# Two orders of work exchanged in the first stage of a four-layer kernel: scores ahead of projections, sigmoids ahead of masked copies

## What is computed

```python
q = (x @ wq.T).reshape(B, T, H, HD)
kv = (x @ wkv.T).reshape(B, T, H, 2 * HD)
nb_k, nb_v = ...   # keys and values of the 16 tokens before
tau = sigmoid(einsum('bthd,bthwd->bthw', q, nb_k) / SCALE)
msg = einsum('bthw,bthwd->bthd', tau, nb_v)
y = x + msg.reshape(B, T, D) @ wo.T
out = (y - mu) * rsqrt(var + LN_EPS) * gamma + beta
```

## Time and profile before

| | us |
|---|---|
| three runs | 1069.3, 1071.47, 1071.88 |
| median | 1071.47 |
| the profiled execution, its own time | 1073.75 |
| its span | 1071.9 |
| PE busy (share) | 887.4 (83%) |
| DVE busy | 671.8 (63%) |
| ACT busy | 572.0 (53%) |
| POOL busy | 492.8 (46%) |

### The profile page before, as it was taken

One profiled execution on the slowest core, in us unless ns is written; L12 is line 12 of the kernel. 1 busy time (PEld: TensorE's weight loads), 2 busy tenths in 40 slices (PEclk: granted clock), 3 DMA queues, 4 the chain that ended last, 5 costly groups with the idle time before them and its releaser, 6 DMA issues.

```text
span 1071.9 us, 21820 instructions
## 1 busy us (share of the span) xinstructions
PE 887.4 (83%) x8032; PEld 712.3 (66%) x8032; DVE 671.8 (63%) x2014; ACT 572.0 (53%) x1033; POOL 492.8 (46%) x893
## 2 busy tenths in 40 slices
PE   1777778276999999998657888998849999999995
PEld 0766667165888888877535565655537888878785
DVE  3566665366588888875329998989856155180622
ACT  1434343133667666665366897977826354362631
POOL 1366665322255455434368899999840002020111
PEclk9856565555789999999867998888959999999998
DMA  9100000110000000000020000000000000000000
GB/s 307 39 10 15 10 15 17 40 50 1 2 6 12 7 12 6 12 12 11 10 84 1 1 1 1 1 1 0 2 0 1 1 1 20 1 20 0 1 20 20
DMA packets 30707, 20.67 MB, mean 19 GB/s; under 512 B 2960, under 2 KB 28952, under 8 KB 30368
## 3 DMA queue, kind: packets, MB, share of 16 engines
q1 hardware_dynamic: 25984, 12.59, 4.1%
q10 hardware_dynamic: 4640, 6.99, 1.9%
HBM read 13.28 MB, written 6.29 MB: 18 GB/s over the span
## 4 chain that ended last, share of the span: by engine, by line
PE 57%; POOL 19%; DVE 10%; issue 6%; ACT 5%; DMA 1%; ACTq 1%; POOLq 0%; SPq 0%; DVEq 0%
PE ps L1108 12%; PE ps L1109 9%; PE ps L1110 9%; PE ps L1121 6%; PE ps L1183 6%; POOL prod L529 5%; POOL term L514 4%; PE ps L1442 3%; PE ps L1176 2%; PE ps L1127 2%; PE ps L1103 2%; POOL c_ln_rs L119 2%; DVE wall L985 2%; POOL a_ln_rs L113 1%; PE ps L1160 1%
## 5 line engine op out<-in xcount | busy, mean ns | idle before, releaser
L112 POOL TENSOR_TENSOR d_ln_ve<-d_ln_mv,eps 128x4 f32<-128x4 f32 x16 | 3.2, 202 | 238.7 <-DVE d_ln_mv L106 238.7
L1108 PE MATMUL ps<-h_h,wh_h 128*128 128x512 f32 x256 | 99.6, 389 | 0.0
L1109 PE MATMUL ps<-h_h,wh_l 128*128 128x512 f32 x256 | 99.6, 389 | 0.0
L1110 PE MATMUL ps<-h_l,wh_h 128*128 128x512 f32 x256 | 99.6, 389 | 0.0
L1183 PE MATMUL ps<-w_e,he 128*128 128x128 f32 x512 | 83.3, 300 | 5.1 <-ACT he L618 4.8
L1121 PEld LDWEIGHTS ps<-mov,hbd 32*128 32x128 f32 x2048 | 85.4, 251 | 0.0
L1121 PE MATMUL ps<-mov,hbd 32*128 32x32 f32 (+1 forms) x2048 | 83.1, 324 | 0.0
L618 ACT ACTIVATE he<-ps,pp 128x256 f32<-128x256 f32 x128 | 59.8, 472 | 43.1 <-PE ps L1110 38.1
L1183 PEld LDWEIGHTS ps<-w_e,he 128*128 128x128 f32 x512 | 73.1, 211 | 7.7 <-ACT he L618 7.0
L529 POOL TENSOR_TENSOR prod<-bcT 16x256 f32<-16x256 f32 (+7 forms) x128 | 69.0, 567 | 6.3 <-ACT bcT L738 6.3
L1086 DVE TENSOR_TENSOR d_y<-ps,w_s 128x512 f32<-128x512 f32 x8 | 5.5, 691 | 102.5 <-PE ps L1442 102.5
(11 more groups left out here) (244 smaller groups left out, 2624.0 us busy)
## 6 DMA issues: line engine op xcount, KB each, us to landing
x<-x SPq DMA_DIRECT2D x32, 128.0 KB, 1.8
x<-in_x SPq DMA_DIRECT2D x16, 128.0 KB
w_h<-in_w_h ACTq DMA_DIRECT2D x2, 1024.0 KB, 8.7
xB<-x SPq DMA_DIRECT2D x32, 64.0 KB
x<-xB SPq DMA_DIRECT2D x32, 64.0 KB
out_x<-x SPq DMA_DIRECT2D x8, 256.0 KB, 2.3
w_m<-in_w_m ACTq DMA_DIRECT2D x3, 256.0 KB, 5.3
xB<-in_w_e ACTq DMA_DIRECT2D x1, 512.0 KB
```

Of the source, the lines that this page charges most:

```text
L1108: pe.matmul(dst, a_h, b_h, start=start, stop=True, skip_group_check=True)
L1109: pe.matmul(dst, a_l, b_h, start=False, stop=True, skip_group_check=True)
L1110: return pe.matmul(dst, a_h, b_l, start=False, stop=True, skip_group_check=True)
```

## The change

On ACT the sigmoids of sequence n now stand ahead of the masked copies of n+1. On PE the scores of n stand ahead of the projection of n+1. The fourth bank of the scores of n holds the transposed input of n+1 until ACT and DVE have made `xh` and `xl` from it, so the wait for `a_xl` now stands ahead of the scores too. No instruction besides this wait is added, and none is removed.

```diff
--- before.py
+++ after.py
@@ -589,10 +589,6 @@
 
 
             def step_a(n, l, have):
-                if have(1):
-                    act.wait_ge(S["a_qk_ps"], n + 2)
-                    four_heads(1 - l, 4 * (1 - l) + 1, S["a_hbd"])
-                    act.activation(mov[1 - l][:, :], ps[:, 4 * (1 - l), 0:NT], ACT.Copy).then_inc(S["a_qT"], 1)
                 if have(0):
                     for k in range(2):
 
@@ -600,6 +596,10 @@
                         act.activation(tau[l][:, 2 * k:2 * k + 2, :],
                                        ps[:, 4 * l + 2 * k:4 * l + 2 * k + 2, 0:NBLK * SPAN], ACT.Sigmoid,
                                        scale=ATT_SCALE).then_inc(S["a_tau"], 1)
+                if have(1):
+                    act.wait_ge(S["a_qk_ps"], n + 2)
+                    four_heads(1 - l, 4 * (1 - l) + 1, S["a_hbd"])
+                    act.activation(mov[1 - l][:, :], ps[:, 4 * (1 - l), 0:NT], ACT.Copy).then_inc(S["a_qT"], 1)
                 if have(2):
                     transposed(l, 4 * (1 - l) + 3, n + 3, S["a_t_ps"], S["a_xh"])
                 if have(0):
@@ -1130,14 +1130,14 @@
 
             def step_a(n, l, have):
                 o = 1 - l
-                if have(1):
-                    pe.wait_ge(S["a_xl"], n + 2)
-                    project(o, 4 * o, wa_h, wa_l, S["a_qk_ps"], S["a_v_ps"])
                 if have(0):
                     pe.wait_ge(S["a_qT"], n + 1)
                     pe.wait_ge(S["a_hbd"], n + 1)
 
                     pe.wait_ge(S["a_vbd"], n + 1)
+                    if have(1):
+
+                        pe.wait_ge(S["a_xl"], n + 2)
                     for g in range(G):
 
                         pe.matmul(bank(l, g, 0, NBLK * SPAN), rep[heads(g), :], band[heads(g), :], start=True, stop=True)
@@ -1147,6 +1147,9 @@
                             last = score(l, bank(l, g, SPAN * j, SPAN * j + w), g, j, w)
                             if j == NBLK - 1 and g % 2 == 1:
                                 last.then_inc(S["a_s_ps"], 1)
+                if have(1):
+                    pe.wait_ge(S["a_xl"], n + 2)
+                    project(o, 4 * o, wa_h, wa_l, S["a_qk_ps"], S["a_v_ps"])
                 if have(2):
                     if have(-1):
```

## The result

The changed kernel takes 1067.65 us (median of 12 runs, 1064.1 to 1072.2), the kernel before, run beside it, 1070.86 us (12 runs, 1067.29 to 1074.64). The ratio is 0.9963, with a 95% interval of 0.9946 to 0.9980: 2 to 6 us less. The forecast was 1069.0 against 1071.47, a ratio of 0.9977.

What follows compares the result with a forecast made beforehand. Two loops were taken to compete: DVE with POOL (10.00 us a step) and PE's path, longer at low clock. Start 37.75 plus steps 134.1 gave 171.8 against 174.32, -2.5 us, end 0: 1069.0 us, range 1065.3 to 1073.8.

Steps and rivals of the forecast that it cites:

- The wait on `xl`: PE's wait, now ahead of the scores too, costs nothing new: the projection ahead of them already waited for it.
- the sigmoids hide under the projection: At low clock ACT's sigmoids run under PE's projection, taking 1.51 us and two handovers off the path, adding 0.69 of transposes.
- T+10.1: With T the start of `t_y`: when PE's path would allow the next `t_y` at low clock, instead of T+10.94.
- ACT's copies behind the sigmoids: Masked copies end about T+7.9, before `msgT` is needed at T+8.4; cost nothing, covered by PE's messages.
- `values` is the price: On DVE at low clock vT waits until T+6.17 for the later projection, statistics start at T+7.78, step becomes 10.51 us.
- `t_z` and vbd come apart: At low clock POOL's `t_z` ends before DVE's vbd begins, paying back about half of what `values` waits.
- rival C: Slower: low clock throughout and vbd keeps 1.49 us, so steps of 10.78 us, 1075.4 us in all; chance 0.12.
- The clock: Scores get less high clock: 5 of 13 steps at 10.00 us, 8 at 10.51, 134.1 us against 135.7.
- Rival B: The high clock stays: all 13 steps at 10.00 us, 1064.3 us in all; chance 0.2.
- The base: The thirteen steps of the kernel before, taken from one profile as 135.70 us, 10.44 us each.
- The start: First scores need only the second sequence's `xl`, so the first `t_y` comes at 37.75 against 38.62: 0.87 us earlier.
- The end: From the `t_y` at 174.32 to the last at 191.87: no change expected, bounds -0.6 and +0.3 us.

Runs made afterwards that it cites:

- e4: Changed kernel with `values` moved on DVE between the third statistics and `t_o`; 1061.49 us, ratio to before 0.9904.
- e2: Kernel before with only ACT's new order (sigmoids ahead of the masked copies), PE's order kept; ratio to before 1.0029.
- e3: Changed kernel with vT reading a constant tile, so `values` wait for nothing (attention's values left out); ratio to before 0.9932.
- e9: Changed kernel run again without alteration, for a second profile; ratio to before 0.9973.
- e11: Against e4: vT moved ahead of the third statistics, vbd alone left behind them; 1068.4 us, ratio to before 0.9957.
- e8: Changed kernel with five extra matmuls on PE behind each output product; ratio to before 0.9964.
- e10: Repetition of e4, unaltered; 1060.77 us, ratio to before 0.9891.
- e7: Kernel before with only `values` moved on DVE behind the third statistics; ratio to before 0.9993.
- e6: Changed kernel with the first stage's projections cut from nine matmuls to three; ratio to before 0.9945.
- e5: Kernel before with the first stage's projections cut from nine matmuls to three; ratio to before 0.9952.

## Why the prediction was right, and where its terms were off

The forecast of -2.5 us lies in what was measured (2 to 6 us less), and 1067.65 us lies in the range of 1065.3 to 1073.8. That range also holds the 1071.47 of no change, so it says little by itself; the steps say more:

- **The wait on `xl` costs nothing**, and **the sigmoids hide under the projection**: as told. The output is ready early, and the wait before `t_y` is gone from the loop. PE's path was even shorter than I reckoned: 9.7 to 9.8 us in e4 where I had T+10.1. I had counted the projection to the end of its last matmul (2.28 us) and the transposes with 0.69, where 2.09 and 0.56 pass until the next instruction starts (111.82, 113.91, 114.47).
- **ACT's copies behind the sigmoids** cost nothing: PE's wait for `msgT` is 0.50 us as before. e2 shows what they cost when PE's order does not cover them.
- **`values` is the price**: as told, shown by e3. vT at T+6.25 against T+6.17, the statistics at T+7.88 against T+7.78, the low-clock step 10.48 to 10.59 against 10.51. That `t_z` and vbd come apart was right: vT is 1.57 us later than before, the third statistics only 0.6. With it rival C (10.78 us) fell. One reading behind it was wrong, though not the number: `t_z` does not lengthen vbd. It is POOL's product before it that does (last section), and that one, too, is over in the long step.
- **The clock**: 5 of 13 short steps expected, 7 and 6 found; 134.1 us expected and 133.5 measured in both profiles. Rival B, all steps at 10.0, did not come. Whether the change itself shifts the share of the high clock stays open: 6 and 9 of 13 steps were short before, 7 and 6 are now.
- **The base was mis-sized.** The thirteen steps of before took 135.7 us in the profile I had and 133.3 in a second. The steps' share of the gain, from the means of two profiles each, is 134.5 - 133.5 = 1.0 us and not 1.6, and the 2.4 us between the two profiles of before are more than that. What is firm is the length by kind: a low-clock step behind a high-clock one took 10.94 us (10.60 to 10.71 where its projection began at the high clock) and takes 10.5 to 10.6. A second low-clock step in a row took 10.40 (from 163.92) and takes 10.49 (e9, from 57.38): there the change gains nothing.
- **The start was mis-sized**: 0.87 us expected, 12.90 - 11.22 = 1.7 us measured (12.89 - 11.34 = 1.6 in the second pair). I had carried over the output's 1.26 us, the projection's 2.28 and the transposes' 0.69. The clock rose before the output product, which took 0.75 us to `t_y`; the transposes began 2.09 us after the projection, and the messages 0.56 us after them. In e11, where the clock did not rise, the start is 11.74, still 1.2 us less than before.
- **The end was mis-sized**: 0 expected, with -0.6 as bound; 24.29 and 22.45 us measured against 24.66 and 25.06, 0.4 and 2.6 less, on average 1.5. The last step, from the fifteenth `t_y` to the sixteenth, was PE's and took 8.48 us in both profiles of before; it takes 6.94 in both of the changed kernel, by DVE and POOL's chain. The last scores start at T+9.18 of the fourteenth `t_y` in the first profile (178.83 against 169.65), near my T+9.35, and at T+6.92 in e9 (177.31 against 170.39), both times at the high clock. At the low clock (e11) they leave a last step of 7.84 us and an end of 24.95, no shorter than before. So the gain at the end hangs on the clock. Four more profiles of the new order, e3, e4, e8 and e10, have ends of 22.28 to 22.74.

So start, steps and end gave about 1.6, 1.0 and 1.5 us, 4.1 in all, against 0.9, 1.6 and 0. Three of the four microseconds came once, from filling and draining the pipeline, and not from the loop, where I had looked for most of the gain. That the sum was off by only 1.6 us is partly luck: the steps were taken too high, the start and the end too low. The split itself rests on two profiles each; only the start is the same in both. I had given 0.36 to a gain of 0.3% or more and 0.52 to no such difference; 0.37% and 0.27% were measured, one on either side.

## What to carry to other kernels

Where two loops of nearly the same length compete, shortening one is worth only the difference between them; here that was 0.4 us a step at best, and only where a low-clock step followed a high-clock one. But it can be the condition for the next step: the same DVE move was worth nothing before (e7) and 6 to 9 us on top of the change (e4, e10). Look for such a follow-up in the engine that now waits, and place work of VectorE so that it does not start just ahead of a small instruction of GpSimd on which the chain hangs (e11). Reckon the start and the end of a pipeline as carefully as its steps: with sixteen sequences they gave more than the loop. And take a second profile of the kernel before, if the argument rests on the share of steps at either clock.

## What the runs showed of the hardware

- A small GpSimd instruction (128x2) that starts 0.17 us after a VectorE product with two SBUF inputs took 1.08 us instead of 0.20 and ended with it (e11). That agrees with what the Trainium skill says (SBUF — State Buffer, "Who interferes with whom"): the first to start keeps the port, the other blocks. The other way round it depends on GpSimd's instruction. In e4 its power (128x2, L113, 92.53, 0.71 us) started ahead of vbd (92.55), which took 1.25 us, hardly more than the 1.22 alone, where the rule would give some 1.9 (an estimate: 0.69 until the power ends, then 1.22).
- A GpSimd product (128x256) that is still running does hold vbd up. In e6 both neighbours of vbd come at other times than in the kernel before:

```profile
91.04 0.72 POOL L428 TENSOR_TENSOR t_zn<-t_zn,rows 128x256 f32<-128x256 f32 x1 [0.93 <-DVE t_zn L135]
...
91.65 1.23 DVE L801 TENSOR_TENSOR vbd<-vT,vmask 128x1024 f32<-128x1024 f32 x1
...
91.84 1.62 POOL L429 TENSOR_TENSOR t_z<-t_zn,rows 128x256 f32<-128x256 f32 x1
```

```profile
101.05 0.72 POOL L428 TENSOR_TENSOR t_zn<-t_zn,rows 128x256 f32<-128x256 f32 x1 [0.93 <-DVE t_zn L135]
...
101.57 1.28 DVE L801 TENSOR_TENSOR vbd<-vT,vmask 128x1024 f32<-128x1024 f32 x1
```

L428 ends 0.11 us after vbd's start in the first, 0.20 in the second and 0.42 in the kernel before (137.92 against 137.50), and vbd takes 1.23, 1.28 and 1.49 us, against 1.22 alone. `t_z` runs beside it all three times and is itself slowed (1.62, 1.59, 1.59), but with vbd at 1.23 it costs vbd nothing. So the 1.49 that the prediction put down to `t_z` is L428's. Its row in the kernel before:

```profile
137.19 0.73 POOL L428 TENSOR_TENSOR t_zn<-t_zn,rows 128x256 f32<-128x256 f32 x1 [0.93 <-DVE t_zn L135]
```

- The column of the granted clock can be wrong in a profile. In e11 it reads 1.00 over the whole stage while the projections' matmuls take 0.41 us and the band's 0.51, as at 0.50 in the others:

```profile
108.00:112.00 4.00, 3.19 (x57) 1.00 0.11 33
```

```profile
109.26 0.51 PE L1150 MATMUL ps<-band,rep 32*128 32x384 bf16 x4 [0.81 <-DVE xl L796]
```

e5 and e6 read 1.00 in the same way, with bands of 0.51 us in every step. The matmuls' own durations are the safer reading, and the mean clocks of e5, e6 and e11 (0.92 to 0.93) are not to be compared with the others.
